# Cross-attention and feed-forward layer: eight buffers of masked scores for six, half a landing buffer of the context, its low halves on VectorE, the first K by chunks and the last h by quarters

## What is computed

```
q = w8a8(layernorm(x), wq);  k = ctx @ wk.T + bk;  v = ctx @ wv.T + bv      # ctx: 16 x 375 x 512
scores = q @ k.T / sqrt(32) + mask;  attn = softmax(scores)                 # 16 heads of 32, 112 x 375 each
x1 = x + w8a8(attn @ v, wo)
h = gelu(int8_matmul(rowquant(layernorm(x1)), W1) + B1)                     # 2048 columns
out = x1 + int8_matmul(rowquant(h), W2) + B2
```

## Time and profile before

| what | us |
|---|---|
| median of 3 runs | 663.83 |
| lowest, highest | 659.75, 665.29 |
| the profiled execution | 658.58 |
| its span in the trace | 656.4 |

### The profile page before, as it was taken

How to read it: one execution, slowest core, us unless ns; L and a number is a source line. 1 busy time by engine, 2 the same in 40 slices (tenths; PEclk the granted TensorE clock), 3 DMA queues, 4 the chain that set the end, 5 groups by cost and what they waited for, 6 DMA issues and landing times.

```text
span 656.4 us, 15000 instructions
## 1 busy us (share of the span) xinstructions
PE 638.5 (97%) x5204; PEld 470.9 (72%) x5204; DVE 474.1 (72%) x1175; ACT 461.1 (70%) x1156; POOL 223.6 (34%) x455
## 2 busy tenths in 40 slices
PE   8898999999999999999999989999999999999999
PEld 4667787777777777768777777877777786767534
DVE  4989788767676766876775834775688768777874
ACT  3545676777887667787687867786777778879702
POOL 3343343252527153530525243341444252321100
DMA  9965865523252443413214253217145231413020
GB/s 313 248 193 143 274 115 175 118 45 80 53 116 61 61 87 61 96 37 79 76 40 85 64 73 40 64 50 124 26 94 60 74 70 27 51 36 74 9 49 33
DMA packets 80586, 58.68 MB, mean 89 GB/s; under 512 B 57984, under 2 KB 67968, under 8 KB 79872
## 3 DMA queue, kind: packets, MB, share of 16 engines
q1 hardware_dynamic: 63680, 31.73, 20.5%
q10 hardware_dynamic: 16832, 25.99, 18.6%
HBM read 41.85 MB, written 3.68 MB: 69 GB/s over the span
## 4 chain that ended last, share of the span: by engine, by line
PE 75%; DVE 11%; DMA 5%; issue 4%; POOL 3%; ACT 2%; ACTq 0%; DVEq 0%; SPq 0%; POOLq 0%
PE ps_ring L1070 32%; PE ps_t L1104 12%; PE ps_s L1097 7%; PE ps_ring L1176 7%; PE ps_t L1116 6%; PE ps_ring L1189 6%; PE ps_ring L1138 2%; PE ps_ring L1063 1%; DMA w_q<-in_w1T 1%; PE ps_s L1165 1%; DVE cols L843 1%; PE ps_ring L1126 1%; DMA yqT<-o_q 1%; DMA x_in<-in_x 1%; DVE probs L872 1%
## 5 line engine op out<-in xcount | busy, mean ns | idle before, releaser
L872 DVE CUSTOM_DVE_ANT_0 probs<-ps_s,mask_in 112x375 f32<-112x375 f32 x256 | 129.6, 544 | 67.8 <-PE ps_s L1097 54.9
L690 ACT ACTIVATE probs<-probs,neg_max 112x375 f32<-112x375 f32 x256 | 154.5, 607 | 27.1 <-DVE neg_max L872 24.6
L700 ACT ACTIVATE pT<-ps_t 125x336 f32<-125x336 f32 x256 | 109.8, 446 | 70.6 <-PE ps_t L1104 64.7
L1104 PEld LDWEIGHTS ps_t<-ident,probs 112*125 112x125 f32 x768 | 107.9, 188 | 42.3 <-issue 18.6
L1104 PE MATMUL ps_t<-ident,probs 112*125 112x112 f32 x768 | 119.9, 278 | 5.6 <-ACT oT L707 2.4
L609 POOL TENSOR_TENSOR ctx_lo<-ctx_in,ctx_hi 128x376 fp32r<-128x376 f32 x60 | 63.8, 1071 | 124.7 <-ACT ctx_hi L668 124.6
L1070 PE MATMUL ps_ring<-ctx_hi,wk_hi 128*128 128x376 f32 x256 | 90.7, 354 | 1.2 <-DVE wk_lo L765 0.7
L1070 PE MATMUL ps_ring<-ctx_hi,wk_lo 128*128 128x376 f32 x256 | 85.5, 334 | 0.0
L1070 PE MATMUL ps_ring<-ctx_lo,wk_hi 128*128 128x376 f32 x256 | 85.4, 334 | 0.0
L1070 PE MATMUL ps_ring<-wv_hi,ctx_hi 128*125 128x512 f32 x192 | 79.1, 412 | 2.0 <-DVE o L882 1.0
L1070 PE MATMUL ps_ring<-wv_lo,ctx_hi 128*125 128x512 f32 x192 | 75.8, 395 | 0.0
(11 more groups left out here) (131 smaller groups left out, 1034.5 us busy)
## 6 DMA issues: line engine op xcount, KB each, us to landing
ctx_in<-in_ctxT ACTq DMA_DIRECT2D x32, 375.0 KB, 4.0
h<-in_w2T SPq DMA_DIRECT2D x4, 1024.0 KB, 5.9
b_row<-in_w2T SPq DMA_DIRECT2D x4, 1024.0 KB, 6.8
x_in<-in_x ACTq DMA_DIRECT2D x16, 224.0 KB, 5.0
xres<-in_x ACTq DMA_DIRECT2D x14, 256.0 KB, 2.6
out<-y ACTq DMA_DIRECT2D x14, 256.0 KB, 2.0
mask_in<-in_mask ACTq DMA_DIRECT2D x16, 164.1 KB, 3.1
w_q<-in_w1T SPq DMA_DIRECT2D x2, 1024.0 KB, 11.3
```

The source lines that it names most:

```text
L690: nc.scalar.activation(probs[:, hd % SP_RING, :], probs[:, hd % SP_RING, :], ACT.Exp, scale=-1.0, bias=neg_max[:, b % 2, hd:hd + 1], accum ...
L700: nc.scalar.activation(pT[0:LR, hd % PT_RING, :], att_bank("T", b, hd)[0:LR, 0:LC * N], ACT.Copy).then_inc(pT_s, 1)
L872: nc.vector.tensor_tensor_reduce(out=probs[:, hd % SP_RING, :], in0=ps_s[hd % HG][0:N, 0:L], in1=mask_in[:, b % 2, :], scale=-1.0, scalar= ...
L1104: last = nc.tensor.transpose(bank[0:LR, lc * N:(lc + 1) * N], probs[:, hd % SP_RING, lc * LR:(lc + 1) * LR], ident[0:N, 0:N])
```

## The change

- `SP_RING` goes from 6 to 8, and the wait of VectorE's S is the same for all heads: the transposition of the head eight before it, across the border of two batches too.
- `ctx_in` holds two chunks instead of four. Both halves of a batch land in the same place, so that `ctx_load` waits until ScalarE and VectorE have split the half before.
- All `ctx_lo` subtractions are VectorE's. GpSimd has none left.
- The first K (unit `k0`) goes by chunks of the contraction, all four groups of columns in the four `ps_s` banks, so that it can begin with the first chunk.
- The last h is rounded, transposed, copied and multiplied by quarters: VectorE takes quarters 0, 1, 2, ScalarE quarter 3; the transposes go to `ps_s1`, `ps_s2`, `ps_s3` and `ps_t0`; `down` takes the quarters in the order 0, 3, 1, 2.
- All five tables are new. Fillers: 13 units in the first part and 19 in the last, none behind the last `down`. wq is loaded first.

The diff, cut to its core (the tables are shown as rows below it):

```diff
-SP_RING = 6
+SP_RING = 8
...
-        ctx_in = sb("ctx_in", [P, KC, LP])
+        ctx_in = sb("ctx_in", [P, KC // 2, LP])
...
-            def split_lo(b, i):
-                if b == 1 and i == 0:
-                    pool.wait_ge(ctx_lo_s, 4)
-                pool.wait_ge(ctx_hi_s, 4 * b + i + 1)
-                wait_for(pool, k_pe, 4 * (b - 1))
-                wait_for(pool, v_pe, 3 * (b - 1))
-                nc.gpsimd.tensor_tensor(ctx_lo[:, b % 2, i, :], ctx_in[:, i, :], ctx_hi[:, b % 2, i, :].bitcast(FP32),
-                                        ALU.subtract).then_inc(ctx_lo_s, 1)
-
             def x_quant(b, i):
...
                     act.wait_ge(pads_ready, 1)
-                act.wait_ge(ctx_in_s[i // 2], 16 * (b + 1))
+                act.wait_ge(ctx_in_s, 16 * (2 * b + i // 2 + 1))
                 wait_for(act, k_pe, 4 * (b - 1))
                 wait_for(act, v_pe, 3 * (b - 1))
-                nc.scalar.activation(ctx_hi[:, b % 2, i, :], ctx_in[:, i, :], ACT.Copy).then_inc(ctx_hi_s, 1)
+                nc.scalar.activation(ctx_hi[:, b % 2, i, :], ctx_in[:, i % 2, :], ACT.Copy).then_inc(ctx_hi_s, 1)
...
                 wait_for(act, scores, 4 * (b - 1))
-                nc.scalar.activation(k_sb[:, b % 2, g, :], bank_of("k", b, g)[:, 0:LP], ACT.Identity,
+                bank = ps_s[g] if b == 0 else bank_of("k", b, g)
+                nc.scalar.activation(k_sb[:, b % 2, g, :], bank[:, 0:LP], ACT.Identity,
                                      bias=bk_col[:, g:g + 1]).then_inc(k_s, 1)
...
-                rows = h[:, F // 2:F]
+                first = 3 * C if t == LAST else F // 2
+                rows = h[:, first:F]
                 act.wait_ge(h_r_s, t + 1)
                 wait_for(act, hT_s, 32 * t)
-                nc.scalar.activation(h_q[:, F // 2:F], rows, ACT.Identity, bias=round_down[:]).then_inc(h_quant_s, 1)
+                nc.scalar.activation(h_q[:, first:F], rows, ACT.Identity, bias=round_down[:]).then_inc(h_quant_s, 1)
+                if t == LAST:
+                    act.wait_ge(down_pe, t)
+                    for bank, j, count in ((ps_s[2], 3, 4), (ps_s[3], 1, 5)):
+                        act.wait_ge(last_T, count)
+                        nc.scalar.activation(hT[:, 4 * j:4 * j + 4, :].rearrange("p k n -> p (k n)"), bank[:, 0:C // 2].bitcast(BF16), ACT.Copy
+                                             ).then_inc(hT_act, 1)
             def load_ctx(b, i):
-                act.dma_start(ctx_in[:, 2 * i:2 * i + 2, 0:L], ctxT[b, 2 * i * P:2 * (i + 1) * P, :].rearrange("(k p) l -> p k l", p=P)
-                             ).then_inc(ctx_in_s[i], 16)
+                act.dma_start(ctx_in[:, :, 0:L], ctxT[b, 2 * i * P:2 * (i + 1) * P, :].rearrange("(k p) l -> p k l", p=P)
+                              ).then_inc(ctx_in_s, 16)
             def ctx_load(b, i):
-                if b >= 1:
-                    act.wait_ge(ctx_lo_s, 4 * (b - 1) + 2 * i + 2)
-                    act.wait_ge(ctx_hi_s, 4 * (b - 1) + 2 * i + 2)
+                wait_for(act, ctx_lo_s, 4 * b + 2 * i)
+                wait_for(act, ctx_hi_s, 4 * b + 2 * i)
                 load_ctx(b, i)
...
                 dve.wait_ge(scores, 4 * b + hd // HG + 1)
-                wait_for(dve, pT_pe, 16 * b + hd + 1 - SP_RING if hd >= SP_RING else 16 * b)
+                wait_for(dve, pT_pe, 16 * b + hd + 1 - SP_RING)
                 if hd == 0:
...
             def h_T(t, i):
-                wait_for(dve, down_pe, t)
-                last_evac(hT[:, 8 * i:8 * i + 8, :], "h_T", i, 8, hT_last)
+                if i == 0:
+                    wait_for(dve, down_pe, t)
+                    dve.wait_ge(last_T, 3)
+                    nc.vector.tensor_copy(hT[:, 0:4, :].rearrange("p k n -> p (k n)"), ps_s[1][:, 0:C // 2].bitcast(BF16)).then_inc(hT_dve, 1)
+                    h_quarter(2)
+                else:
+                    dve.wait_ge(last_T, 6)
+                    nc.vector.tensor_copy(hT[:, 8:12, :].rearrange("p k n -> p (k n)"), ps_t[0][:, 0:C // 2].bitcast(BF16)).then_inc(hT_dve, 1)
             def split_lo(b, i):
-                dve.wait_ge(ctx_hi_s, i + 1)
-                nc.vector.tensor_tensor(ctx_lo[:, 0, i, :], ctx_in[:, i, :], ctx_hi[:, 0, i, :].bitcast(FP32), ALU.subtract
+                dve.wait_ge(ctx_hi_s, 4 * b + i + 1)
+                wait_for(dve, k_pe, 4 * (b - 1))
+                wait_for(dve, v_pe, 3 * (b - 1))
+                nc.vector.tensor_tensor(ctx_lo[:, b % 2, i, :], ctx_in[:, i % 2, :], ctx_hi[:, b % 2, i, :].bitcast(FP32), ALU.subtract
                                         ).then_inc(ctx_lo_s, 1)
...
                 wait_for(dve, hT_s, 32 * b)
-                round_rows(b, h[:, 0:F // 2], h_r, h_q[:, 0:F // 2], h_round_lo, h_quant_lo, h_r_s)
+                if b == LAST:
+                    dve.wait_ge(h_r_s, b + 1)
+                    h_quarter(0)
+                    h_quarter(1)
+                else:
+                    round_rows(b, h[:, 0:F // 2], h_r, h_q[:, 0:F // 2], h_round_lo, h_quant_lo, h_r_s)
+
+            def h_quarter(j):
+                part = slice(j * C, (j + 1) * C)
+                nc.vector.tensor_scalar(h[:, part], h[:, part], h_r, ROUND, ALU.mult, ALU.add).then_inc(h_round_lo, 1)
+                dve.wait_ge(h_round_lo, LAST + 1 + j)
+                nc.vector.tensor_scalar(h_q[:, part], h[:, part], -ROUND, None, ALU.add).then_inc(h_quant_lo, 1)
...
             def k_unit(b, g):
-                if b == 0:
-                    pe.wait_ge(w_lo, 2)
                 pe.wait_ge(ctx_lo_s, 4 * (b + 1))
                               lambda k: ctx_hi[:, p, k, :], lambda k: ctx_lo[:, p, k, :]).then_inc(k_pe, 1)
+
+            def k_first(b, k):
+
+                pe.wait_ge(w_lo, k // 2 + 1)
+                pe.wait_ge(ctx_lo_s, k + 1)
+                for g in range(KC):
+                    cols = slice(g * P, (g + 1) * P)
+                    for t, (w, c) in enumerate(((wk_hi, ctx_hi), (wk_hi, ctx_lo), (wk_lo, ctx_hi))):
+                        last = nc.tensor.matmul(ps_s[g][:, 0:LP], w[:, k, cols], c[:, 0, k, :],
+                                                start=(k == 0 and t == 0), stop=(k == KC - 1 and t == 2))
+                    if k == KC - 1:
+                        last.then_inc(k_pe, 1)
...
+            def quarter_T(bank, j):
+                for n in range(4):
+                    k = 4 * j + n
+                    last = nc.tensor.transpose(bank[:, n * P // 2:(n + 1) * P // 2].bitcast(BF16), h_q[:, k * P:(k + 1) * P], ident_bf[:])
+                last.then_inc(last_T, 1)
+
             def h_T(t, i):
-                pe.wait_ge((h_quant_lo, h_quant_s)[i], t + 1)
-                rows_T("h_T", i, h_q, 8, 8 * i)
+
+                if i == 0:
+                    pe.wait_ge(masked, 16 * B)
+                    pe.wait_ge(h_quant_lo, LAST + 1)
+                    quarter_T(ps_s[1], 0)
+                    pe.wait_ge(h_quant_s, LAST + 1)
+                    quarter_T(ps_s[2], 3)
+                    pe.wait_ge(h_quant_lo, LAST + 2)
+                    quarter_T(ps_s[3], 1)
+                else:
+                    pe.wait_ge(oT_s, 4 * OT_DONE[B])
+                    pe.wait_ge(h_quant_lo, LAST + 3)
+                    quarter_T(ps_t[0], 2)
                 for _ in range(WARM):
-                    nc.tensor.matmul(ps_s[0][:, :], ident_bf[:], warm_row, start=True, stop=True)
+                    nc.tensor.matmul((ps_t, ps_s)[n][0][:, :], ident_bf[:], warm_row, start=True, stop=True)
...
             def down(b, i):
+                quarter = i
+                if b == LAST:
+                    quarter = (0, 3, 1, 2)[i]
+                    pe.wait_ge(*((hT_dve, 1), (hT_act, 1), (hT_act, 2), (hT_dve, 2))[i])
+                elif i == 0:
+                    pe.wait_ge(hT_s, 32 * (b + 1))
                 if i == 0:
-                    if b == LAST:
-                        pe.wait_ge(hT_last, 2)
-                    else:
-                        pe.wait_ge(hT_s, 32 * (b + 1))
                     pe.wait_ge(w_quant, 8)
                 for n in range(4):
-                    k = 4 * i + n
-                    last = nc.tensor.matmul(bank, hT[:, k, :], w2_q[:, k, :], start=(k == 0), stop=(k == FK - 1))
+                    k = 4 * quarter + n
+                    last = nc.tensor.matmul(bank, hT[:, k, :], w2_q[:, k, :], start=(i == 0 and n == 0), stop=(i == 3 and n == 3))
                 if i == 3:
-            units = {"w_T": w_T, "so": so, "w_max": w_max_unit, "q": q, "k": k_unit, "v": v_unit, "S": S, "T": T, "PV": PV, "gather": gather,
+            units = {"w_T": w_T, "so": so, "w_max": w_max_unit, "q": q, "k0": k_first, "k": k_unit, "v": v_unit, "S": S, "T": T, "PV": PV, "gather": gather,
                      "o_T": o_T, "out_proj": out_proj, "y_T": y_T, "up": up, "h_T": h_T, "down": down, "warm": warm}

```

310 lines of the change are left out of this document (156 added, 154 removed).

## The result

The changed kernel took 670.38 us in the median of 8 runs (667.11 to 675.45), the kernel before, beside it, 661.29 (659.75 to 665.29): a ratio of 1.0155, 95% interval 1.0128 to 1.0182. It is slower: the medians lie 9 us apart, and by the ratio, which I use from here on, it is 10 us, where 7.2 us less were forecast. 670.38 is outside both the forecast's own range (652 to 660.5) and its wider one (648 to 667). The profiled execution took 668.3 us, its span 666.5.

A forecast was written before the change was run, and what follows sets the result against it. It took VectorE and one transfer to bound the start, PE the middle, and a chain into fillers the end; -2.0 - 2.6 - 2.6 = -7.2 us from the median 663.83 gave 656.6, range 652 to 660.5.

The forecast's parts named there:

- Start: Up to about 115 us, following VectorE: -2.0 us, bounds -6 and +4.
- four subtractions at 0.547: VectorE, first pass over wq to end of wo's rounding: subtractions added as 2.19 us of work, in a 27.5 us sum.
- under that wait: Wait on w1's last quarter, 9.43 or 5.9 us: VectorE does q, two subtractions, second x and three heads of scores meanwhile.
- bound of +4 for the start: Worst case: wq at 10.3, w1's quarter taking 9.43 us, and the second half of the first context late.
- this part, -2.0: First rounding pass over w1 to end of batch 0's scores: -2.1 + 1.1 - 1.0 = -2.0 us, from 25.5 before.
- the passes over w2 that follow: 75 to 115 us: less crowding by GpSimd's subtractions continues, another -0.5 us.
- VectorE becomes the late engine: Rival, batches 0 to 2: subtractions delay context loads, ScalarE's queue, K and V; +7.4 us, 671.2, chance 0.14.
- Middle: 75 to 600 us: two more buffers recover a third of PE's 7.9 us idle, -2.6 us; ends -9 and +7.
- The rule on the shared port: Middle: VectorE's two-SBUF-input subtractions would lose to GpSimd on the port lock, 7.3 us more; forecast then 658.4, not 656.6.
- End: Last h by quarters, no fillers behind the last down: -2.6 us, bounds -3.5 and -1.0.
- PE's stand before the first K: Start: PE idle some 3 us for wq's rounding, free while VectorE is later; over 4 us would show the forecast wrong.
- The other two signs: Signs of a wrong forecast: PE's waits on ctx_lo or K grow; ScalarE sits idle at a load of ctx_in.

The follow-up runs named there:

- own_memory: The changed kernel, with the second halves of the first two contexts landing in idle memory (hT, oT) so their loads issue early; 1.0016 of the kernel before.
- own_memory's twin: As own_memory, but the load of batch 1's x stays where the changed kernel has it in ScalarE's order; 1.0049 of the kernel before.

## Why the forecast was wrong

**Start: the step that failed.** The sum along VectorE put batch 1's first two subtractions in as work, two of the "four subtractions at 0.547", and gave nothing for a wait ahead of them; the next two it hid "under that wait" on w1's last quarter. They were a wait: for a load that can't be issued before the subtractions of batch 0 (26.31) and then needs 13.3 us. The forecast named that chain as a rival, and its bound of +4 for the start even named a late half of a context, but of batch 0; batch 1's was priced nowhere, and I never worked out when it could be issued. The change's own wait, that a half lands only behind the subtractions of the half before, gave the earliest issue (in the trace 16.3 us behind the first pass over wq, so some 24 us with the forecast's 8 for that pass), and w1's last quarter took 9.43 us in such a stretch already before the change. For a term of -2.0 the first gather shows +10.6, of which the landing is 7.2 (own_memory).

In own_memory, where the landing is early, wo's rounding ended at 36.8 against the forecast 35.5, but that is two errors against each other: the first pass over wq began at 11.95 for the forecast's 8 (10.00 in the changed kernel: wq had landed as forecast, but the first x's statistics and two subtractions stand ahead in VectorE's order), and the stretch from there took 24.9 us for 27.5. The first pass over w1 came at 53.1 for 49.5, with three masks and a pass ahead of it. From there to the end of batch 0's scores it took 22.3 us in both kernels, for the forecast's 23.5 and 25.5 before: this part, -2.0, was right in sign and came out a little better.

A second term failed as well: "the passes over w2 that follow" were put at -0.5, and from the last mask of batch 0 to the first gather it took 3.4 us more than before, 2.6 even in own_memory. What stands there is the late quarter of w2; that it is the cause was not tested.

**The rival that came nearest** is "VectorE becomes the late engine": 671.2 forecast, 670.4 measured, with a chance of 0.14. Its mechanism holds in half: subtraction, load, ScalarE's queue. But it put +4 at the start and +6 in the middle; measured +10.6 and +1.1. The agreement of the sums is luck (and of two levels: the rival counts +7.4 from a median of 663.83, the measurement +10 from 661.29), and "VectorE late" is the wrong name: VectorE was idle for 8.2 us at that landing and free enough for its 64 subtractions.

**Middle.** Forecast -2.6. The changed orders took 510.8 to 518.4 us between the gathers in twelve kernels' single executions, those of before with six buffers 511.4 to 514.0 in three, so a trace of one execution can't settle 2.6 us. With the start repaired own_memory, whose orders in the middle are the changed kernel's, had 512.58, 1.5 less than before. A buffer less in it cost 1 to 3 us, the subtractions back on GpSimd about as much, and a seventh buffer in the kernel before gave 0.9983. All three point the way that was forecast, but each is at the edge of what the intervals can tell or inside it (against own_memory's twin two of them are 1 us), so neither the sign nor the size of -2.6 is shown.

**The rule on the shared port.** A subtraction took 546 ns in the median, at most 1032, and the mean of the page's group was 569: 64 x 0.023 = 1.5 us more in all, not the 7.3 (for 52 of them) that the rule of the Trainium skill (page "SBUF — State Buffer", section "SBUF: two separate sides") would have made by my reckoning. In the trace each of the five records with a long subtraction has a GpSimd operation beside it (the one of 1032 ns began at 447.96, beside an addition from 447.29 to 448.59), but fifteen records of normal length have one too. So the long ones fit the rule, and the loss that I worked out from it was five times too large. And o's rounding still had its 1575 ns, though no subtraction is GpSimd's now, so its long case wasn't the subtractions' doing.

**End.** -2.1 by the rows for -2.6, within -3.5 and -1.0. From h's scale to the last down it was 6.7 us, where the forecast had 6.4 and before 7.6: the mechanism was right and the term 0.5 too large.

**PE's stand before the first K** "costs nothing as long as VectorE is the later one": so it was, as far as the timed runs tell. It was 4.65 us, over the 4 that the forecast had as a sign of trouble, and neither fillers in it nor, from own_memory, a first K 4.3 us earlier made the timed runs faster. The other two signs were the true ones: ScalarE was idle for 9.64 us at a load of `ctx_in`, and PE for 6.80 with ctx_lo named (by the kernel's waits it was the eviction behind the same landing). The assumption that failed beside them was a granted clock of 1.00 throughout: it was 0.66 and 0.63 behind the stands, a mix of the 1.2 and 2.4 GHz levels. That cost at most 1.2 us here.

## What to carry to other kernels

When a landing buffer is cut, work out for the first rounds when each load can be issued at the earliest (the last reader of the half before) and add the landing time of the busiest stretch, not the median over the run; then look at what stands behind the first reader in every in-order queue, and at what stands ahead of the last reader of the half before, since that sets the issue. A buffer that is needed whole only while the weights load can borrow memory that is idle then. Parts of a bundled change are priced one by one: here two of them gained 0.35% together (0.13 to 0.58) and the third cost three to four times that. A path that is repaired at one place is followed on: the next late load may stand 40 us further.

## What the runs showed of the hardware that was not expected

- The same 375 KB load took a median of 3.6 us over the run and 13.3 us when issued at 26.31, beside 1 MB of w1, a broadcast and the transposition of x (which took 9.2 us). From 20 to 42 us the queues moved 146 GB/s in the mean, with 1136 of 1990 packets under 512 bytes; from 8 to 32 us of before it was 292 GB/s. But such a load was slow there too, 11.0 us in the median of three:

```profile
ctx_in<-in_ctxT ACTq DMA_DIRECT2D x3, 375.0 KB, 11.0
```

What the change made worse was less the landing than its issue, 26.31 for 9.49, which left nothing to hide it. Changing who goes first moved the landing by 1.5 us only. Which of the small packets slow the rest wasn't separated.
- PE came back from stands of 4.65 and 6.80 us with a granted clock of 0.66 (15 to 20 us) and 0.63 (40 to 45 us), and fillers kept it at 1.00. The first gather gained 1.2 us by it and the timed runs nothing: where PE's work waits for others anyway, a low clock costs little.
